# Two-layer mixed transformer: projection in token layout with gates as rows, and row scores two at a time on the halves of the array's rows

## The reference

```python
# layer 0: graph attention (16 heads, the first 20 tokens as keys), then
x = exp_v + relu(output)
# layer 1: a transformer block with modulation from the condition
ada = silu(cond) @ ada_w.T + ada_b            # gamma1, gamma2, scale1, scale2, shift1, shift2
x1 = _ln(x) * (scale1 + 1) + shift1
q, k, v = split(x1 @ mat_qkv_w.T + qkv_bias)  # 16 heads of 16 channels
q = _l2norm(q) * sm ; k = _l2norm(k)
o = softmax(q @ k.T) @ v
x = x + (o @ proj_w.T + proj_b) * gamma1      # the part that is changed
x2 = _ln(x) * (scale2 + 1) + shift2
x = x + (gelu(x2 @ fc1_w.T + fc1_b) @ fc2_w.T + fc2_b) * gamma2
```

## Time and profile before

| | us |
|---|---|
| median of 3 runs (811.96 to 813.43) | 813.35 |
| time of the profiled execution | 811.12 |
| its span, first to last instruction | 809.4 |
| PE busy | 751.6 |
| DVE busy | 480.5 |
| ACT busy | 461.6 |
| POOL busy | 308.9 |
| mean granted clock of TensorE (share of full) | 0.976 |

### The profile page before, as it was taken

The page is one execution under the profiler, slowest core; times in us unless marked ns, Lnnn a source line. Parts: engine busy times, 40 slices in busy tenths (PEclk is TensorE's granted clock), DMA queues, the critical chain, the costliest instruction groups (busy, mean ns, idle before and its releaser), DMA issues.

```text
span 809.4 us, 15270 instructions
## 1 busy us (share of the span) xinstructions
PE 751.6 (93%) x4800; PEld 533.2 (66%) x4800; DVE 480.5 (59%) x1031; ACT 461.6 (57%) x780; POOL 308.9 (38%) x533
## 2 busy tenths in 40 slices
PE   4789999999996799999999999999888999999997
PEld 2578788888863355555555555555556888888885
DVE  2158998998997656665555655555413544344432
ACT  0335555455542376777777777776556555555553
POOL 1025555555553254444444444444432112222100
PEclk9889999999999699999999999999989999999999
DMA  8831242433304777776677777777600000000001
GB/s 243 289 99 46 85 125 78 123 115 87 103 19 89 133 130 126 129 131 127 125 126 120 124 124 124 126 124 131 110 1 1 14 14 26 27 27 28 14 26 40
DMA packets 80763, 75.44 MB, mean 93 GB/s; under 512 B 22671, under 2 KB 71439, under 8 KB 80719
## 3 DMA queue, kind: packets, MB, share of 16 engines
q1 hardware_dynamic: 79390, 74.73, 43.0%
q10 hardware_dynamic: 1328, 0.16, 0.1%
HBM read 52.94 MB, written 21.63 MB: 92 GB/s over the span
## 4 chain that ended last, share of the span: by engine, by line
PE 56%; ACT 5%; issue 2%; DVE 2%; POOL 1%; ACTq 0%; POOLq 0%
PE ps L1650 11%; PE ps L1664 11%; PE ps L1468 7%; PE ps L1540 6%; PE ps L1526 6%; PE ps L1578 3%; PE ps L1476 3%; PE ps L1493 3%; ACT probsT L884 2%; PE ps L1559 2%; ACT part_pairs L913 2%; PE ps L1460 1%; PE ps L1679 1%; PE ps L1510 1%; ACT projT L905 1%
## 5 line engine op out<-in xcount | busy, mean ns | idle before, releaser
L884 ACT ACTIVATE probsT<-ps 128x1024 f32<-128x1024 f32 x128 | 130.9, 1022 | 44.7 <-PE ps L1526 42.3
L1285 DVE TENSOR_TENSOR hidden_low<-hidden,hidden_high 128x512 fp32r<-128x512 f32 x64 | 46.5, 726 | 107.7 <-ACT hidden_high L987 59.3
L1187 DVE TENSOR_REDUCE neg_max<-ps 128x4 bf16<-128x344 f32 x128 | 63.9, 509 | 57.0 <-PE ps L1493 56.3
L984 ACT ACTIVATE hidden<-ps,b_fc 128x512 f32<-128x512 f32 x64 | 44.1, 690 | 70.5 <-PE ps L1650 70.5
L1526 PEld LDWEIGHTS ps<-q_stack,k_stack 49*128 49x128 f32 x512 | 39.2, 189 | 65.0 <-issue 32.9
L1540 PE MATMUL ps<-probsT,v_ones 128*32 128x256 f32 x1024 | 69.2, 388 | 4.1 <-ACT probsT L884 4.1
L1526 PE MATMUL ps<-q_stack,k_stack 49*128 49x256 f32 x512 | 65.8, 336 | 7.1 <-ACT probsT L884 7.0
L681 POOL TENSOR_TENSOR scores<-scores,row_max 128x640 f32<-128x640 f32 x32 | 42.1, 1316 | 76.8 <-DVE row_max L1025 76.8
L1468 PE MATMUL ps<-w_qkv,x1T 128*128 128x512 f32 x128 | 65.3, 635 | 2.8 <-DVE part_pairs L1194 2.8
L1386 PE MATMUL ps<-x_res,w_q 128*128 (+1 forms) x256 | 65.2, 400 | 0.0
L1386 PEld LDWEIGHTS ps<-x_res,w_q 128*128 128x128 f32 x256 | 48.5, 199 | 11.5 <-issue 5.5
(11 more groups left out here) (176 smaller groups left out, 1757.8 us busy)
## 6 DMA issues: line engine op xcount, KB each, us to landing
parts_dram<-part_pairs SPq DMA_DIRECT2D x64, 256.0 KB
q_stack<-parts_dram SPq DMA_DIRECT2D x96, 128.0 KB, 5.4
k_stack<-parts_dram SPq DMA_DIRECT2D x96, 128.0 KB, 6.3
adj<-in_adj SPq DMA_DIRECT2D x16, 440.0 KB, 3.5
xT<-in_xT SPq DMA_DIRECT2D x16, 256.0 KB, 2.6
x_res<-in_x SPq DMA_DIRECT2D x16, 256.0 KB, 3.5
x_in<-in_x SPq DMA_DIRECT2D x16, 256.0 KB, 2.6
out_x<-result SPq DMA_DIRECT2D x16, 256.0 KB, 2.1
```

The costliest lines, as they stand in the source:

```text
L884: nc.scalar.activation(probsT[:, s % 4, :], ps[:, COLS:COLS + 2, :].rearrange("p a n -> p (a n)"), ACT.Exp).then_inc(exp_made, 1)
L984: nc.scalar.activation(hidden[:, s % RAW, :], ps[:, FC1[s % FC1_BANKS], :], ACT.Gelu, bias=b_fc1[:, m:m + 1]).then_inc(gelu_made, 1)
L1187: nc.vector.tensor_reduce(neg_max[:, tt, at:at + 4], ps[:, ROW_BANKS[n % 2], 0:4 * KP].rearrange("p (a g) -> p a g", a=4), AX_X, ALU.max, ...
L1285: nc.vector.tensor_tensor(hidden_parts[1][:, s % H_SLOTS, :], hidden[:, s % RAW, :], hidden_parts[0][:, s % H_SLOTS, :], ALU.subtract).the ...
```

## The change

The projection is made with the o channels as stationary side, so that its result has tokens on the partitions. The gate gamma1 and the gated bias are then rows, the same for every token: `gate_rows_made` transposes the columns of all 16 batches once in turn 1, ScalarE copies them to SBUF, SP stores them in DRAM (`rows_dram`), and at the end of each turn `get_rows` fetches the row of the next projection to all 128 partitions (one DMA, 256 KB, after put_low). VectorE multiplies by the gate (`gate`), GpSimd adds the bias to x_res (`bias`, between `roots` and `blocks_of_pairs`), VectorE adds the two (`residual`). ScalarE's gate and TensorE's residual are gone.

Row scores are now four pairs, in slots 1 to 4: each matmul of a pair has 64 rows of the array and four heads' places, and writes a bank of its own. `key_blocks` has four places instead of eight. The maxima of all 16 heads are transposed and taken at once, in slot 5 after `project`, and there is one `max_row` per turn (two DMAs of 8 heads' rows). `unit_qk` stands first in its slot on VectorE, `output_tokens` ahead of `norm_transposed` on TensorE. In setup the offset's four small loads become one. The FFN part gets the last batch's gate and residual on VectorE at steps 4 and 5.

```diff
...
-    GROUPS = 8
-    GROUPS_AT = ((), (0,), (1,), (2,), (3,), (4,), (5,), (6,), (7,), ())
+
+    GROUPS = 4
+    GROUPS_AT = ((), (0,), (1,), (2,), (3,), (), (), (), (), ())
     VALUES = (3, 4, 7, 9)
     QK_BANK, PV_BANK, SIDE, COLS = 2, 0, 5, 6
     ROW_BANKS = (4, 1)
     MAX_BANK = ROW_BANKS[1]
+    MAX_AT = 5
     def groups(b, s):
         return () if b is None else GROUPS_AT[s]
-
-    def group_of(n):
-        return n // 4, n // 2 % 2, n % 2
     @block.sync
     def _(sp):
...
         turns(graph_turn, sp, 3)
-        def max_row(b, par, i):
-            sp.wait_ge(m_out, 2 * b + i + 1)
+        def max_row(b, par):
+            sp.wait_ge(m_out, b + 1)
             for c in range(C2):
                 at = HALF * c + KROWS
-                sp.dma_start(q_stack[at:at + 1, par, 4 * i:4 * i + 4].bitcast(F32), neg_maxT[4 * c:4 * c + 4, i, :].bitcast(F32)).then_inc(m_row_in[i], 16)
+                sp.dma_start(q_stack[at:at + 1, par].bitcast(F32), neg_maxT[HT * c:HT * c + HT, :].bitcast(F32)).then_inc(m_row_in, 16)
         def put_high(n, par):
             for w in range(2):
...
             fetch(q_stack, par, Q_PARTS.index(1), 0, 1)
             fetch(k_stack, par, K_PARTS.index(1), 1, 1)
+        def get_rows(d):
+
+            if isinstance(d, int) and d == 0:
+                sp.wait_ge(rows_stored, 16)
+            ge(sp, gated_made, d)
+            ge(sp, biased, d)
+            sp.dma_start(gate_rows[:], rows_dram[bass.ds(d, 1), :].rearrange("o e -> (o e)").partition_broadcast(P)).then_inc(rows_in, 16)
+
         def turn(f, b, c, d, par):
-            if c is not None:
-                max_row(c, par, 1)
             if b is not None:
                 get_high(b, 1 - par)
                 get_low(b, 1 - par)
-                max_row(b, 1 - par, 0)
+                max_row(b, 1 - par)
             if f is not None:
                 ge(sp, stack_in, f * FETCHED)
                 put_high(f, par)
                 put_low(f, par)
+            if isinstance(f, int) and f == 1:
+                sp.wait_ge(rows_out, 1)
+                sp.dma_start(rows_dram, gated[0:B, :]).then_inc(rows_stored, 16)
+            if c is not None:
+                get_rows(c)
         sp.wait_ge(x_made, B - 2)
...
             nc.gpsimd.tensor_tensor(sums[:, :, KP - 1], sums[:, :, KP - 1], keys[:, :, N - 3], ALU.add).then_inc(pairs_made, 1)
             pool.wait_ge(pairs_made, 4 * f + 4)
             for k in range(C2):
-                nc.gpsimd.tensor_tensor(key_blocks[:, par, k], key_sums[:, k * KP:(k + 1) * KP].unsqueeze(1).broadcast_to([P, HT, KP]),
-                                        row_head[:].unsqueeze(2).broadcast_to([P, HT, KP]), ALU.mult).then_inc(blocks_made, 1)
+                nc.gpsimd.tensor_tensor(key_blocks[:, par, k], key_sums[:, k * KP:(k + 1) * KP].unsqueeze(1).broadcast_to([P, HT // 2, KP]),
+                                        row_head[:].unsqueeze(2).broadcast_to([P, HT // 2, KP]), ALU.mult).then_inc(blocks_made, 1)
+
+        def bias(d):
+            pool.wait_ge(rows_in, 16 * (d + 1))
+            pool.wait_ge(xhat_made, T * (d + 1))
+            x = x_res[:, bass.ds(d * T, T), :]
+            nc.gpsimd.tensor_tensor(x, x, gate_rows[:, F:2 * F].unsqueeze(1).broadcast_to([P, T, F]), ALU.add).then_inc(biased, 1)
         def turn(f, b, c, d, par):
             ahead = following(f)
...
             if f is not None:
                 if not isinstance(f, int) or f >= ROOTS_ON_VECTOR:
                     roots(f)
+            if d is not None:
+                bias(d)
+            if f is not None:
                 blocks_of_pairs(f, par)
             if isinstance(c, int) and c == B - 2:
                 pool.wait_ge(g["late_weights"], g["LATE"])
...
             nc.scalar.activation(v_ones[:, par, :, :, 0:HD], halves(ps, SIDE).rearrange("p t (h d) -> p t h d", d=HD),
                                  ACT.Copy).then_inc(v_out, 1)
-        def take_maxima(b, i):
-            act.wait_ge(m_mm, 2 * b + i + 1)
-            ge(act, m_row_in[i], 32 * b)
-            nc.scalar.activation(neg_maxT[:, i, :], ps[0:HT, MAX_BANK, 0:N // 2].bitcast(BF16), ACT.Identity,
-                                 bias=place_offset[:, i:i + 1]).then_inc(m_out, 1)
+        def take_maxima(b):
+            act.wait_ge(m_mm, b + 1)
+            ge(act, m_row_in, 32 * b)
+            nc.scalar.activation(neg_maxT[:], ps[0:H, MAX_BANK, 0:N // 2].bitcast(BF16), ACT.Identity, bias=place_offset[:, 0:1]).then_inc(m_out, 1)
         def probabilities(c, s):
             act.wait_ge(st_mm, 8 * c + s + 1)
...
             for k in range(C2):
                 nc.scalar.activation(oT[:, k, :], halves(ps, SIDE)[:, k, :], ACT.Identity, bias=b_v[:, k:k + 1]).then_inc(ot_out, 1)
-        def gate(d):
-
-            act.wait_ge(proj_mm, d + 1)
-            ge(act, res_mm, d)
-            if isinstance(d, int):
-                ge(act, gated_bias, C2)
-            for k in range(C2):
-                nc.scalar.activation(projT[:, k, :], halves(ps, SIDE)[:, k, :], ACT.Identity, bias=b_gated[:, k, bass.ds(d, 1)],
-                                     scale=ada[:, k, bass.ds(d, 1)]).then_inc(proj_out, 1)
+        def take_rows():
+            act.wait_ge(rows_mm, 1)
+            nc.scalar.activation(gated[0:B, :], ps[0:B, SIDE, :], ACT.Copy).then_inc(rows_out, 1)
         def high(f, par):
             ge(act, parts_out, 2 * 16 * (f - 1))
...
                 if following(f) is not None and s == 4:
                     shift_scale(following(f), 1 - par)
                 if isinstance(c, int) and c == B - 1 and s == 0:
-                    take_maxima(c, 1)
                     act.wait_ge(s_mm, GROUPS * B)
                 if c is not None and s < 8:
                     probabilities(c, s)
                 if isinstance(c, int) and c == B - 1 and s < C2:
                     ffn_scale(0, (s,))
-                if c is not None and s == 0 and not (isinstance(c, int) and c == B - 1):
-                    take_maxima(c, 1)
                 if d is not None and s == 4:
                     add_bias_v(d)
-                if b is not None and s == 5:
-                    take_maxima(b, 0)
                 if c is not None and s == 5:
                     take_sums(c, 0)
-                if d is not None and s == 6:
-                    gate(d)
+                if isinstance(f, int) and f == 1 and s == 6:
+                    take_rows()
+                if b is not None and s == MAX_AT:
+                    take_maxima(b)
                 if f is not None and s == 6:
                     high(f, par)
             if c is not None:
...
                                     root[0][:].unsqueeze(2).broadcast_to([P, HH, HD]), ALU.mult).then_inc(qkn_made, 1)
         def maxima(b, n):
-            j, k, tt = group_of(n)
-            if n % 4 == 0:
-                ge(dve, m_mm, 2 * (b - 1) + j + 1)
+            k, tt = n // T, n % T
+            if n == 0:
+                ge(dve, m_mm, b)
             dve.wait_ge(s_mm, GROUPS * b + n + 1)
-            at = HT * j + 4 * k
-            nc.vector.tensor_reduce(neg_max[:, tt, at:at + 4], ps[:, ROW_BANKS[n % 2], 0:4 * KP].rearrange("p (a g) -> p a g", a=4), AX_X, ALU.max,
-                                    negate=True).then_inc(max_made, 1)
+            for j in range(2):
+                at = HT * k + 4 * j
+                nc.vector.tensor_reduce(neg_max[:, tt, at:at + 4], ps[:, ROW_BANKS[j], 0:4 * KP].rearrange("p (a g) -> p a g", a=4), AX_X, ALU.max,
+                                        negate=True).then_inc(max_made, 1)
         def rests(f, par):
             for w in range(2):
...
                                         denom[:, tt, :].rearrange("p (h c) -> p h c", c=C2).unsqueeze(3).broadcast_to([P, HT, C2, HD]),
                                         ALU.mult).then_inc(otok_made, 1)
+        def gate(d):
+            dve.wait_ge(proj_mm, d + 1)
+            dve.wait_ge(rows_in, 16 * (d + 1))
+            nc.vector.tensor_tensor(gated[:].rearrange("p (t f) -> p t f", t=T), halves(ps, SIDE), gate_rows[:, 0:F].unsqueeze(1).broadcast_to([P, T, F]),
+                                    ALU.mult).then_inc(gated_made, 1)
+
         def residual(d):
-            dve.wait_ge(res_mm, d + 1)
+            dve.wait_ge(gated_made, d + 1)
+            dve.wait_ge(biased, d + 1)
             x = x_res[:, bass.ds(d * T, T), :].rearrange("p t f -> p (t f)")
-            nc.vector.tensor_tensor(x, ps[:, SIDE, :], x, ALU.add).then_inc(res_made, 1)
+            nc.vector.tensor_tensor(x, gated[:], x, ALU.add).then_inc(res_made, 1)
         def turn(f, b, c, d, par):
             ahead = following(f)
             for s in range(SLOTS):
+                if f is not None and s == 5:
+                    unit_qk(f)
                 for n in groups(b, s):
                     maxima(b, n)
                 if ahead is not None and s == 0:
...
                     roots(f)
```

(64 more changed lines are left out.)

56 lines of the change are left out of this document (28 added, 28 removed).

## The result

The changed kernel takes 798.86 us in the median (796.66 to 799.76, 4 runs), the kernel before 812.81 us; the ratio is 0.9825, with a 95% interval of 0.981 to 0.984. The prediction said 798.

A forecast was written before the change was run, and what follows sets the result against it. It took the transfer loop, 20.0 us against an engines' chain of 19.4, to set the turn; 11.9 + 2.5 + 0.8 = 15.2 us off the profiled 811.1 gave 796, or 798 for the median, range 790 to 809.

The forecast's parts named there:

- What bounds the kernel: Attention turns of 20.88 us: TensorE up to the transposes after col_scores 6, then ACT; transfer loop a second bound at 19.3.
- ACT: Last quarter of a turn: gate leaves the chain, saving 0.90 us, with unit_qk and split_qk no later.
- The array: TensorE's part of a turn: 0.16 for a row score, 0.15 for max_transposed, 0.25 for norm_transposed's wait; 0.56 us saved.
- Whether a pair costs as much as one ... I take 0: Row scores, slots 1 to 4: a half-height pair costs no more than one matmul; other end 0.64 us a turn.
- The half-height mode is the one that col_scores just before it uses, so I add nothing for a change of it: Row-score pairs on the array: no added cost for changing mode, since col_scores just before is half-height too.
- DVE and POOL: Bias on POOL starts when unit_qk does on DVE: 0.55 us a turn if bias goes first, 0 if unit_qk does.
- C: Rival, chance 0.25: dearer engines' chain, by pairs (+0.64) or bias (+0.55); turns of 20.0 to 20.6, 799 to 806 us.
- Loop: 19.3 + 0.7 = 20.0 us. This is longer than 19.4, so the loop sets the turn.: Put_high, fetches, landing: the row load adds 0.7 us to the loop, exceeding the engines' chain and setting the turn.
- held SP ahead of the fetches: SP's queue: the max_row removed each turn had held SP until ACT's maxima at the turn's start; no size given.
- A: Rival, chance 0.4: the transfer loop sets the turn at about 20.0 us, giving 798 us.
- B: Rival, chance 0.2: the row load is hidden in idle DMA time; turn 19.4 us, giving 791 us.
- which stands behind the last maximum and residual: End of turn 16: PE's 1.40 us wait for x_hat_f goes, since last maximum and residual on DVE come earlier.

The follow-up runs named there:

- high_on_two: Changed kernel with the edits of unit_first and rows_first_end, plus the queries' half of high moved from ACT to DVE: 794.61 us, 0.9761 of the kernel before.
- projection_one_load: Kernel before with only the new projection, bias and gate, the row of batch 0 fetched once for all batches: 798.54 us, 0.9832 of the kernel before.
- pairs_only: Changed kernel with the old projection (gate on ACT, residual's transposes on the array): 808.73 us, 0.9955 of the kernel before.
- unit_first: Changed kernel with POOL's bias made to wait until unit_qk of the same turn is done: 795.96 us, 0.9802 of the kernel before.
- Projection_only: Kernel before with only the new projection, bias, gate and fetched rows, full-height row scores kept: 819.0 us, 1.0074 of the kernel before.
- max_first: Changed kernel with max_transposed between col_scores 5 and project instead of after project: 798.6 us, 0.983 of the kernel before.
- same_half: Changed kernel with both matmuls of each row-score pair reading rows 0 to 63: 806.91 us, 0.9917 of the kernel before.
- rows_first_end: Changed kernel with the row of batch 13 fetched before put_high in turn 15 only: 794.67 us, 0.9796 of the kernel before.

## Why the prediction came out right, and where it was wrong

**What bounds the kernel: right.** The array up to col_scores 6, then ACT: the chain after has the same shape, and high_on_two bears out ACT's part (0.29 us for 0.5 taken off ACT).

**ACT: right.** Gate's 0.90 us: projection_one_load gained 0.87. With one max_transposed gone behind the turn, the part behind col_scores 6 was to lose 1.05; it lost 0.97.

**The array: wrong in size.** The failed step is "Whether a pair costs as much as one ... I take 0", and with it "The half-height mode is the one that col_scores just before it uses, so I add nothing for a change of it". The pair itself is as short as one (0.60 us from col_scores to the group behind it, 0.59 before), but make_v and output_channels behind it are 0.10 and 0.07 us dearer than behind a full-height row score; the second make_qk is so by only 0.02. In slot 5, where I counted 0.16 us for the removed row score, project became 0.11 us dearer and left 0.05. In all the pairs and the transposes' new order won 0.25 us a turn (pairs_only), not 0.56. The wait for take_v did go.

**DVE and POOL: the mechanism right, the price wrong.** Where bias went first, in seven turns of twelve, unit_qk took 2.34 us, which was my condition for C; in the other five it was first and kept its 1.23. I charged 0.55 us a turn; unit_first shows 0.07 in the mean. The delay falls into the time that high spends behind probabilities 6 anyway, which I had allowed for only in part.

**The queue: the failed step is "Loop: 19.3 + 0.7 = 20.0 us. This is longer than 19.4, so the loop sets the turn."** The 19.3 was right for the kernel before, and it is what the loop takes in all four kernels without the load. The 0.7 that I added for the load was wrong in the changed kernel even in its sign: there the loop with the load takes 18.2 us in the mean and without it 19.3, since the fetches land sooner. Of the max_row that leaves SP's queue I said only that it "held SP ahead of the fetches", and gave it no number. By itself it is worth nothing to the loop (19.3 with one and with two); in the two kernels with the load the one with a single max_row has the loop 2.7 us shorter, and these two differ in their row scores as well. So the step that failed is known, and why load and max_row act together like this stays open. Projection_only, with load and both max_rows, ran bound by its loop, as A had it for the whole change.

**The sum.** A turn of 19.78 us lies between B (19.4) and A (20.0), nearest in kind to C: the engines' chain, dearer than I worked out, by the pair's aftermath and hardly by bias. The twelve turns won 2.0 us more than predicted, and the end won nothing of what it was to win: 3.4 + 0.8 predicted, -0.7 and -1.4 in this profile, and about 0 in those of unit_first, max_first and same_half. I had looked at x_hat_f's wait for the DVE queue only ("which stands behind the last maximum and residual"), not at POOL's: bias is ahead of the weights' split and ffn_root there, and waits for a row that is fetched behind put_high. The errors cancelled: that 798 was met is in part luck.

## What to carry to other kernels

When a change adds a transfer to a queue and takes another out of it, the loop can't be had by adding a price for each: here the same load made it 1.6 us longer or 1.1 us shorter. Measure the loop, landing included. The parts tried alone can give the wrong sign (here +0.7% and -0.5%, together -1.8%). An added wait on a queue must be followed to what stands behind it at the ends of the pipeline, where the next stage's work is in the same queue, and not in the full turns alone. Two instructions that lock each other out cost little (0.07 to 0.15 us in a turn here) as long as the later one is hardly what the next engine waits for, and more (0.4 to 0.5) as soon as something else becomes faster. And a mean over turns can hide two kinds of turn: look at them one by one.

## What the hardware showed that was not expected

Two half-height matmuls of 344 columns on the two halves of the rows take no more than one of full height (a pair costs 0.125 us less than with both on one half), yet the full-height group that follows them directly is up to 0.10 us longer than behind a full-height row score (make_v, 1.92 and 1.82 us to the next group). Project directly behind col_scores is as much longer, and two transposes of 16 columns in between don't change it.

POOL's tensor_tensor of 128x512 with two SBUF operands and DVE's of 128x1024 stop each other for nearly their whole length. Whichever starts first, even by 0.01 or 0.03 us, keeps its time (1.27 and 1.23 us), and the other takes 2.33 or 2.34 us. Which it is changed from turn to turn, and with it the length of the turn: 19.71 and 19.85 us.

A gap of the array can cost more than its own length: with the wait of 5.01 us the granted clock was 0.50 for the 16.9 us from 569.30 to 586.20, in which the array was busy for 10.49. With no such wait (rows_first_end) it was at 0.50 for some 6 us only, later on (575 to 581).
